# An LSTM feeding six attention layers: the state h is kept doubled in its history, and halved when a layer reads it

## What is computed

```python
def step(carry, xw_t):
    prev_h, prev_c = carry
    a = xw_t + prev_h @ Wh
    i = jax.nn.sigmoid(a[:, :Hdim])
    f = jax.nn.sigmoid(a[:, Hdim:2 * Hdim])
    o = jax.nn.sigmoid(a[:, 2 * Hdim:3 * Hdim])
    g = jnp.tanh(a[:, 3 * Hdim:])
    next_c = f * prev_c + i * g
    next_h = o * jnp.tanh(next_c)
    return ((next_h, next_c), next_h)
...
for i in range(DEPTH):
    x = attn_layer(shift_tokens(x), Wqkv[i], q_scale[i], k_scale[i], Wo[i]) + x
    x = ffn_layer(shift_tokens(x), ln_g[i], ln_b[i], W1[i], b1[i], W2[i], b2[i]) + x
```

## Time and profile before

| | us |
|---|---|
| median of 3 runs | 5004.61 |
| lowest and highest run | 5001.86, 5004.77 |
| the profiled execution | 5005.17 |
| its span, first to last instruction | 5003.4 |

### The profile page before, as it was taken

The page is one execution under the profiler, slowest core; times in us unless marked ns, Lnnn a source line. Parts: engine busy times, 40 slices in busy tenths (PEclk is TensorE's granted clock), DMA queues, the critical chain, the costliest instruction groups (busy, mean ns, idle before and its releaser), DMA issues.

```text
span 5003.4 us, 192617 instructions
## 1 busy us (share of the span) xinstructions
PE 4830.9 (97%) x80032; PEld 3861.4 (77%) x80032; DVE 3388.5 (68%) x14449; ACT 2622.6 (52%) x8224; POOL 1713.0 (34%) x1982
## 2 busy tenths in 40 slices
PE   8998999999999999999999999999999999999888
PEld 8996787777777777777777778777777777776665
DVE  4445777777777767677777777767677776775554
ACT  2223555555555555555555555555555555556555
POOL 0003333343433333343333433333343333334442
PEclk5557999999999999999999999999999999999999
DMA  4002233223323332332333233233223323324341
GB/s 148 28 28 57 77 93 110 83 89 112 90 77 101 105 86 82 113 94 77 100 103 89 83 116 86 77 110 98 86 82 117 89 77 110 95 87 127 90 129 49
DMA packets 313086, 456.55 MB, mean 91 GB/s; under 512 B 213408, under 2 KB 240672, under 8 KB 298912
## 3 DMA queue, kind: packets, MB, share of 16 engines
q1 hardware_dynamic: 312224, 444.35, 29.3%
HBM read 378.10 MB, written 66.19 MB: 89 GB/s over the span
## 4 chain that ended last, share of the span: by engine, by line
PE 65%; DVE 11%; issue 7%; POOL 4%; ACT 4%; DMA 0%; POOLq 0%; DVEq 0%; SPq 0%; ACTq 0%
PE mm L902 14%; PE gates L185 13%; PE st L1014 8%; PE gates L177 5%; PE dd L1014 4%; PE st L941 4%; PE pt L1041 4%; PE tt L914 3%; PE pt L1049 3%; PE pt L955 3%; DVE qk L1361 2%; POOL va L805 2%; DVE pr L1411 2%; PE dd L971 2%; PE st L983 1%
## 5 line engine op out<-in xcount | busy, mean ns | idle before, releaser
L790 POOL TENSOR_TENSOR turned<-raw,rotl 128x256 f32<-128x256 f32 x768 | 705.6, 934 | 1667.6 <-ACT raw L1133 1358.2
L902 PE MATMUL mm<-wqkv,xa 128*128 128x512 f32 x2304 | 1166.8, 618 | 12.6 <-DMA rot<-in_rotary 8.8
L185 PE MATMUL gates<-hp,whp 128*128 128x6 bf16 x28672 | 849.1, 165 | 22.0 <-DVE hp L230 22.0
L185 PEld LDWEIGHTS gates<-hp,whp 128*128 128x128 bf16 x28672 | 784.3, 96 | 56.7 <-DVE hp L230 29.3
L192 ACT ACTIVATE state<-gsum 128x16 f32<-128x16 f32 x896 | 195.6, 218 | 1011.7 <-DVE gsum L200 1005.4
L1184 ACT ACTIVATE pr<-st,nb,qn 128x128 f32<-128x128 f32 x1536 | 687.5, 464 | 37.2 <-DVE nb L1399 36.7
L902 PEld LDWEIGHTS mm<-wqkv,xa 128*128 128x128 f32 x2304 | 384.5, 193 | 242.2 <-issue 223.1
L200 DVE TENSOR_REDUCE gsum<-gates 128x16 f32<-128x48 f32 x896 | 182.9, 204 | 526.7 <-PE gates L185 526.7
L177 PEld LDWEIGHTS gates<-hp,whp 128*128 128x128 bf16 x14336 | 423.2, 96 | 141.2 <-issue 85.4
L177 PE MATMUL gates<-hp,whp 128*128 128x2 bf16 x14336 | 485.8, 163 | 26.0 <-DVE hp L215 26.0
L798 POOL TENSOR_TENSOR qn<-ss,power 128x8 f32<-128x8 f32 x192 | 326.9, 1703 | 497.1 <-DVE ss L1370 487.8
(11 more groups left out here) (132 smaller groups left out, 9803.4 us busy)
## 6 DMA issues: line engine op xcount, KB each, us to landing
wqkv<-in_Wqkv SPq DMA_DIRECT2D x288, 512.0 KB, 4.3
w<-in_W SPq DMA_DIRECT2D x48, 1364.0 KB, 6.0
wo<-in_Wo SPq DMA_DIRECT2D x48, 1024.0 KB, 4.9
w<-in_W SPq DMA_DIRECT2D x48, 768.0 KB, 4.5
kT<-k_windows SPq DMA_DIRECT2D x96, 256.0 KB, 5.7
va<-v_windows SPq DMA_DIRECT2D x96, 256.0 KB, 5.9
k_windows<-kT SPq DMA_DIRECT2D x96, 256.0 KB, 4.2
v_windows<-vb SPq DMA_DIRECT2D x96, 256.0 KB, 4.8
```

Source lines behind the costliest of these rows:

```text
L185: last = nc.tensor.matmul(g[:, m * PARTS * BATCH:(m + 1) * PARTS * BATCH], self.whp[:, p, k, m * P:(m + 1) * P], self.hp[:, k, :, :].rearr ...
L790: ins = nc.gpsimd.tensor_tensor(dst[:, :, a, :], src[:, :, 1 - a, :], tab[:, :, a, :].broadcast_to([P, 8, HALF]), ALU.mult)
L902: ins = nc.tensor.matmul(mm[c % 2][:, :], shifted(xa, y.b, k), wqkv[:, c, k, :], start=(k == 1), stop=(k == 0))
```

## The change

Every step's full h is written straight into the history, doubled as it is. The second and third part of h are then computed from there. `h_keep` and its semaphore are removed from all steps. `from_history` waits for the count of `h_chain`, which each step raises twice, and multiplies by 0.5 where it copied. The tile h32 stays for the initial state.

```diff
@@ Lstm.__init__
-        self.history = sem("history")
@@ class Lstm
+    def full(self, t):
+
+        return self.hist[:, bass.ds(t, 1), :].rearrange("p a n -> p (a n)")
+
@@ on_dve (first stage)
-        state, uv, hp, h32, oc = self.state, self.uv, self.hp, self.h32, self.OC
+        state, uv, hp, h32, oc = self.state, self.uv, self.hp, self.full(t), self.OC
...
-        nc.vector.scalar_tensor_tensor(h32[:, :], state[:, 0:HC], 1.0, self.tcell[:, :], ALU.add, ALU.mult).then_inc(self.h_chain, 1)
+        nc.vector.scalar_tensor_tensor(h32, state[:, 0:HC], 1.0, self.tcell[:, :], ALU.add, ALU.mult).then_inc(self.h_chain, 1)
...
-        nc.vector.tensor_tensor(hp[:, :, 1, :], pairs(h32[:, :]), hp[:, :, 0, :], ALU.subtract).then_inc(self.h_chain, 1)
-        nc.vector.tensor_tensor(pairs(self.hrest[:, :]), pairs(h32[:, :]), hp[:, :, 0, :], ALU.subtract).then_inc(self.h_rest, 1)
+        nc.vector.tensor_tensor(hp[:, :, 1, :], pairs(h32), hp[:, :, 0, :], ALU.subtract).then_inc(self.h_chain, 1)
+        nc.vector.tensor_tensor(pairs(self.hrest[:, :]), pairs(h32), hp[:, :, 0, :], ALU.subtract).then_inc(self.h_rest, 1)
...
-        nc.vector.tensor_scalar(self.hist[:, bass.ds(t, 1), :].rearrange("p a n -> p (a n)"), h32[:, :], 0.5, None, ALU.mult).then_inc(self.history, 1)
@@ layer stage
     def dve_full(self, nc, dve, t):
-        nc.vector.scalar_tensor_tensor(self.h32[:, :], self.state[:, 0:HC], 1.0, self.tcell[:, :], ALU.add, ALU.mult).then_inc(self.h_chain, 1)
+        nc.vector.scalar_tensor_tensor(self.full(t), self.state[:, 0:HC], 1.0, self.tcell[:, :], ALU.add, ALU.mult).then_inc(self.h_chain, 1)
...
-        nc.vector.tensor_tensor(self.hp[:, :, 1, :], pairs(self.h32[:, :]), self.hp[:, :, 0, :], ALU.subtract).then_inc(self.h_chain, 1)
+        nc.vector.tensor_tensor(self.hp[:, :, 1, :], pairs(self.full(t)), self.hp[:, :, 0, :], ALU.subtract).then_inc(self.h_chain, 1)
...
-        nc.vector.tensor_tensor(pairs(self.hrest[:, :]), pairs(self.h32[:, :]), self.hp[:, :, 0, :], ALU.subtract).then_inc(self.h_rest, 1)
+        nc.vector.tensor_tensor(pairs(self.hrest[:, :]), pairs(self.full(t)), self.hp[:, :, 0, :], ALU.subtract).then_inc(self.h_rest, 1)
...
-    def dve_keep(self, nc, dve, t):
-        nc.vector.tensor_scalar(self.hist[:, bass.ds(t, 1), :].rearrange("p a n -> p (a n)"), self.h32[:, :], 0.5, None,
-                                ALU.mult).then_inc(self.history, 1)
@@ layer_stage, VectorE
             def from_history(c, b):
-                dve.wait_ge(lstm.history, c * TILE + TILE)
+                dve.wait_ge(lstm.h_chain, 2 * (c * TILE + TILE))
                 for k in range(KT):
-                    x_in.inc(nc.vector.tensor_copy(own(xa, b, k), lstm.hist[:, bass.ds(c * TILE, TILE), k * BATCH + b]))
+                    x_in.inc(nc.vector.tensor_scalar(own(xa, b, k), lstm.hist[:, bass.ds(c * TILE, TILE), k * BATCH + b], 0.5, None, ALU.mult))
@@ slot: h_keep() and its eleven calls
-                def h_keep(): one("h_keep", lstm.dve_keep)
...
                 gate_sum()
-                h_keep()
                 row_scale(x, 0)
...
```

## The result

The kernel after takes 4954.46 us (median of 6 runs, 4953.25 to 4956.33), the kernel before 5002.0 us (median of 6 runs, 5000.32 to 5004.77; the three runs that the prediction started from are among them). The ratio is 0.9905, with 95% between 0.9894 and 0.9916: 47.5 us less. The profiled execution has a span of 4952.4 us, where that before had 5003.4: 51.0 us less, of which about 3 are due to the profiled execution before, which lay 3 us above its median.

The account below looks back on a forecast made before the run. TensorE, busy 97% of 5003.4 us, was taken as the bound. From the median of 5004.61 us, -14.6 (Place A) - 10.8 (Place B) + 2 (loop) - 21 (clock) = -44.4 gave 4960 us; range 4944 to about 4992.

Parts of the forecast that it names:

- Place A: Sixth step: the keep, held beside GpSimd, delays the gate sum and h; removal saves 0.19 us in 77 slots, 14.6 us.
- rival 1: GpSimd goes first at Place A, L206 is held through both L790, Place A gives nothing: 4988 us; chance 0.16.
- Place B: Tenth step: two earlier keeps delay L1370, which releases GpSimd's power; removal saves 0.14 us in 77 slots, 10.8 us.
- The seven second slots of a last layer: Sixth step in seven of 84 slots: TensorE late by itself behind a ScalarE mask copy; gain counted at nothing.
- Fifth and eighth step as before: The other two late steps, 0.31 and 0.26 us in the wait list: no keep in their chains, so they stay.
- The loop of the first stage: 20 hardware-loop steps: register operations for the history address enter the h chain, costing 1.1 to 3.4 us; 2 taken.
- The copy that multiplies: 32 copies of 272 ns into the layer input become multiplications: 0 taken, between 3.8 us gain and 7.6 us loss.
- The clock: Layer stage: 25 drops of TensorE to 1.2 GHz, at most 1.7 us each; 12 or 13 fewer, -21 us.
- The rule weighed: VectorE operations with two SBUF inputs or two-port mode exclude GpSimd's, issue order deciding; assumed in Place A, Place B differs.
- the third: Rival of no change: a second cause right behind keeps h as late in both places; 5003 to 5007 us, chance 0.17.
- The second: Rival: gains as forecast, but as many clock drops as before; 4981 us, chance 0.12.
- The fourth: Rival of slower: the new slot length meets more clock drops, losing from 14 additional on; 5023 or 5074 us, chance 0.05.

Follow-up runs that it names:

- pad_14: Kernel after with 14 spare two-column matmuls on TensorE in each slot's third step; 5001.34 us, ratio 0.9999.
- pad_24: Kernel after with 24 spare two-column matmuls on TensorE in each slot's third step; 5040.76 us, ratio 1.0075.
- floor_late: Kernel after with VectorE's rot_floor(y, 2) moved behind h_third in the eighth step; 4941.80 us, ratio 0.9877.
- pow_table: Kernel after with GpSimd's norm(y, 2) ahead of the turns of piece 3 and rot_table between norm(y, 1) and v_copy; 4916.42 us, ratio 0.9827.
- pow_first: Kernel after with GpSimd's norm(y, 2) moved ahead of the turns of piece 3; 4953.63 us, ratio 0.9900.
- put_back_a: Kernel after with one spare multiplication of the keep's form per slot, ahead of the sixth step's gate sum; 4985.98 us, ratio 0.9965.

## Why the prediction was right

4960 us were forecast, 4944 to 4992 as the range, and faster as the likeliest case; 4954.46 was measured. Its steps, one by one:

- **Most keeps lie under TensorE's work.** Right: 644 of them put back cost nothing.
- **Place A, 0.19 us.** Right in size and in its chain (the distances of the sixth step show 0.19). L201 came early, L207 went between the two turns and L211 was held. It was the most uncertain step (rival 1 had L206 held behind both turns), and the row of L207, 0.20 us long, decides it.
- **Place B, 0.14 us.** Right but for 0.02 us: the second distance is 419 ns, not 400.
- **The seven second slots of a last layer.** Counted at nothing; 0.04 us each, 0.3 us in all.
- **Fifth and eighth step as before.** Right; the 84 waits are still there. That no keep was in their chains was right, too. But the eighth is held by a turn just as A was, and that could have been read in the trace of before.
- **The loop of the first stage, 2 us.** Too high, and below the lower bound: one register operation a step is left, as before; it moved from the keep, behind the chain, to the history write, in it, and the two readers need none. The step grew from 2.88 to 2.92 us, 0.8 us in all against at least 1.1. L163 is the history write, DVEq the queue of VectorE:

```profile
L163 DVEq FUSED_REGOPS  x20: 57/57/75, 371.2 to 427.0; - x20
```

- **The upper end of the range.** It is added up wrongly: rival 1 (4988) with the upper bounds of the loop (+1.4) and of the copy (+7.6) is 4997, not 4992. The measured time lies far from this end.
- **The copy that multiplies, zero.** Right: 274 ns (median) where the copy took 272.

```profile
L1296 DVE TENSOR_SCALAR xa<-hist x32: 265/274/281, 433.6 to 4483.5; 128x128 f32<-128x128 f32 x32
```

- **The clock, 12 or 13 drops fewer, -21 us.** The direction was right, the size too small: 16 fewer, 26.2 us. This is the term that was mis-sized, and it makes most of what was missed: 47.5 us by the medians, 51.0 in the profiled executions, against a sum of 44.4; 3.5 drops more are 5.7 us. The price of a drop was well bounded: at most 1.7 us forecast, 1.64 measured. The sign "10 to 15 drops" was just missed, with 9. That shorter slots meet fewer drops was taken from a few stretches of the trace with shorter slots and from the last chunk; pad_14 and pad_24 show it as a rule of this kernel between 48.03 and 48.65 us, floor_late (6 at 47.97) and pow_table (9 at 47.59) show that it ends below. Taking half of the possible effect was a guess between two ends and no derivation, and that the edit's 0.35 us led to fewer drops, and not past the fewest to more again, was luck as far as the prediction goes.
- **190 us less of VectorE's records.** Wrong as it was put: the 896 records of 211 ns are gone, but VectorE's busy time fell by 97 us, since records of small operations overlap and the page counts time in which at least one runs. The prediction's own 0.07 us an operation (63 us) was nearer.
- **The rule weighed.** In A L207, issued before the second turn, went before it, as the order of issue has it (the Trainium skill, page "SBUF — State Buffer", section "Who interferes with whom"). In B the row that differed from it is reproduced: L1370 was issued at 1985.13, before L765 (1985.22), and yet it ends 0.55 us after L765 does (1985.94, 1986.49). In pow_first it ends 0.54 after L765 (2083.82, 2084.36), in pow_table, without L765 behind `v_copy`, 0.55 after `v_copy` (2063.35, 2063.90). So it was L765 that held it. Why L207, L211 or the keep pass between two turns and L1370 doesn't pass between `v_copy` and the table stays open; the kernels differ in size and kind of both operations, and no run separated these.

Of the rivals, the first falls with the row of L207, the third with the stalls that are gone. The second (drops as many as before) would have needed a count that doesn't depend on the slot's length; pad_14 and put_back_a show that it does. The fourth (more drops) did not come: 9 were left of 25. Its premise, that the count hangs on the slot's length, is right, and in pad_24 a longer slot meets more of them.

## What to carry to other kernels

Of 896 small operations on an engine that was not the bottleneck, 252 at most cost everything: look for the ones that are held by GpSimd or stand ahead of what releases it, by going through one period of the work and comparing the distances between matmul groups, since stalls under 0.15 us stand in no list of waits. When a held operation is moved or taken out, ask which operation is held next by the same GpSimd work (floor_late, pow_first), and move the GpSimd work if it can be. And in a kernel whose TensorE is nearly always busy count the stretches at half clock before and after each edit: here, between 48.03 and 48.65 us, they about doubled what every tenth of a microsecond in a slot was worth.

## What the runs showed of the hardware that was not expected

The number of half-clock stretches depends steeply on the length of a slot: 9 at 48.03 us, 16 at 48.19, 25 at 48.38, 32 at 48.65, so that 0.62 us more in each slot, 52 us in all, brought 23 drops, another 38 us. Each costs 1.64 us of its 3.4 (a slot of 48.03 us takes 49.67). The Trainium skill, page "TensorE: Matmul & The Clock Gate", section "Terms", prices throttled time at the share of the clock that is missing, half here, which would be 1.7 us; the rows agree nearly. Padding TensorE with useless matmuls, which made the slot longer, did not lessen the drops but brought more of them. And shorter is not always fewer: 6 drops at 47.97 us, but 9 at 47.59.

An operation of four or eight values a row that takes 0.15 us alone can be held for 0.58 to 0.70 us by one GpSimd operation of 0.72 to 0.73 us (the keep by one of 1.03 us, of which it met the last 0.67): as TENSOR_SCALAR (the keep, the floor), as SCALAR_TENSOR_TENSOR (L211) and as TENSOR_TENSOR (L224), but not as TENSOR_REDUCE.
